# Transformer block on one core: attention with four heads on four TensorE row groups, and full-size matmuls ahead of the loop

## The reference

```python
h = _layernorm(x, axis=-1) * (1 + ca) + sa
x = x + ga * _L0_attn_ref(h, wq, w_down, wk_up, wv_up, wo)
h = _layernorm(x, axis=-1) * (1 + cb) + sb
x = x + gb * _L0_ffn_ref(h, Wg, bg, W1, b1, W2, b2)
```

```python
q = (x @ wq).reshape(B, T, H, D)
lat = x @ w_down
k = (lat @ wk_up).reshape(B, T, H, D)
v = (lat @ wv_up).reshape(B, T, H, D)
scores = jnp.einsum('bqhd,bkhd->bhqk', q, k) * scale
allowed = pages[None, :] <= pages[:, None]
scores = jnp.where(allowed[None, None], scores, jnp.finfo(scores.dtype).min)
attn = jax.nn.softmax(scores, axis=-1)
out = jnp.einsum('bhqk,bkhd->bqhd', attn, v).reshape(B, T, E) @ wo
```

## Time and profile before

| | |
|---|---|
| median of 3 runs | 771.66 us |
| the profiled execution | 771.94 us |
| its span, first to last instruction | 770.1 us |
| TensorE busy | 681.2 us (88%) |
| VectorE busy | 588.5 us (76%) |
| ScalarE busy | 520.4 us (68%) |
| GpSimd busy | 183.8 us (24%) |
| mean granted clock of TensorE | 0.940 |

### The profile page before, as it was taken

The page is one execution under the profiler, slowest core; times in us unless marked ns, Lnnn a source line. Parts: engine busy times, 40 slices in busy tenths (PEclk is TensorE's granted clock), DMA queues, the critical chain, the costliest instruction groups (busy, mean ns, idle before and its releaser), DMA issues.

```text
span 770.1 us, 12222 instructions
## 1 busy us (share of the span) xinstructions
PE 681.2 (88%) x3976; PEld 427.2 (55%) x4000; DVE 588.5 (76%) x1133; ACT 520.4 (68%) x905; POOL 183.8 (24%) x144
## 2 busy tenths in 40 slices
PE   3920988999699999987599999999999999999996
PEld 2410222333233333345478777787777877778885
DVE  5670987888588888229678898888988889888775
ACT  2530035677476777973488888888888888888984
POOL 0451016000000000000223343333433344322322
PEclk9965579999899999998799999999999999999998
DMA  9541041100101000000111110011100111101200
GB/s 237 150 139 65 0 117 40 43 21 25 46 2 44 24 20 4 3 1 1 66 45 55 56 56 28 29 56 56 55 34 24 54 56 57 54 2 55 69 15 28
DMA packets 17413, 37.20 MB, mean 48 GB/s; under 512 B 3305, under 2 KB 11241, under 8 KB 14533
## 3 DMA queue, kind: packets, MB, share of 16 engines
q1 hardware_dynamic: 16037, 34.65, 13.9%
q10 hardware_dynamic: 1312, 1.74, 0.9%
HBM read 31.86 MB, written 4.33 MB: 47 GB/s over the span
## 4 chain that ended last, share of the span: by engine, by line
PE 33%; DVE 12%; issue 5%; ACT 1%; POOL 0%; POOLq 0%; DVEq 0%
DVE gel_lo L1049 6%; PE y L952 6%; PE y L954 5%; PE y L953 5%; PE hid L943 5%; PE hid L942 5%; PE hid L941 5%; PE plog L963 2%; DVE part L1105 1%; ACT gel_hi L1017 1%; DVE at_least L1077 1%; PE pcw L972 1%; DVE cw L1096 0%; DVE cw L1094 0%; DVE dl L1084 0%
## 5 line engine op out<-in xcount | busy, mean ns | idle before, releaser
L1049 DVE TENSOR_TENSOR gel_lo<-gel,gel_hi 128x512 fp32r<-128x512 f32 x256 | 248.3, 1010 | 6.7 <-ACT gel_hi L1017 5.7
L588 DVE TENSOR_REDUCE mcol<-mx 128x1 f32<-128x512 f32 (+2 forms) x320 | 193.1, 635 | 61.7 <-PE mx L704 58.8
L562 ACT ACTIVATE probs<-st 128x512 f32<-128x512 f32 x288 | 155.7, 596 | 99.3 <-PE st L660 57.1
L1016 ACT ACTIVATE gel<-hid,b_sb 128x512 f32<-128x512 f32 x256 | 176.1, 688 | 38.5 <-PE hid L943 16.2
L1017 ACT ACTIVATE gel_hi<-hid,b_sb 128x512 fp32r<-128x512 f32 x256 | 174.7, 682 | 0.0
L1157 POOL TENSOR_TENSOR cur<-cur,part 128x512 f32<-128x512 f32 x64 | 106.4, 1663 | 250.8 <-DVE part L1105 250.8
L704 PE MATMUL mx<-ks,qs 125*128 125x512 bf16 (+3 forms) x384 | 120.8, 364 | 38.3 <-PEq L208 32.0
L952 PE MATMUL y<-gel_hi,w_hi 128*128 128x512 f32 x256 | 104.4, 408 | 0.4 <-DVE gel_lo L1049 0.2
L941 PE MATMUL hid<-cur_hi,w_hi 128*128 128x512 f32 x256 | 102.2, 399 | 0.4 <-DVE cur_lo L1123 0.4
L943 PE MATMUL hid<-cur_hi,w_lo 128*128 128x512 f32 x256 | 102.2, 399 | 0.0
L942 PE MATMUL hid<-cur_lo,w_hi 128*128 128x512 f32 x256 | 102.1, 399 | 0.0
(11 more groups left out here) (147 smaller groups left out, 521.9 us busy)
## 6 DMA issues: line engine op xcount, KB each, us to landing
cwb<-gate_rows SPq DMA_DIRECT2D x16, 1024.0 KB, 4.7
ks<-in_k_rows SPq DMA_DIRECT2D x3, 640.0 KB
qs<-in_q_rows SPq DMA_DIRECT2D x3, 616.0 KB
q_pieces<-pieces_q SPq DMA_DIRECT2D x4, 384.0 KB, 4.8
k_pieces<-pieces_k SPq DMA_DIRECT2D x4, 384.0 KB, 6.0
ks<-k_pieces SPq DMA_DIRECT2D x8, 192.0 KB
qs<-q_pieces SPq DMA_DIRECT2D x8, 192.0 KB
x_sb<-in_x SPq DMA_DIRECT2D x4, 256.0 KB, 5.2
```

The source lines that it names most:

```text
L562: nc.scalar.activation(probs[u % SLOTS][:, h, :], st[:, (HG * u + h) % ST_RING, :], ACT.Exp, scale=SCALE).then_inc(exp_done, 1)
L588: nc.vector.tensor_reduce(mcol[a % SLOTS][:, h, slot:slot + step * (len(blocks) - 1) + 1:step], mx[:, at % MX_RING, 0:len(blocks) * keys]. ...
L1016: nc.scalar.activation(gel[n % RING][:, :], hid[n % RING][:, :], ACT.Gelu_apprx_tanh, bias=bias)
L1049: nc.vector.tensor_tensor(gel_lo[n % RING][:, :], gel[n % RING][:, :], gel_hi[n % RING][:, :], ALU.subtract).then_inc(lo_ok, 1)
```

## The change

A group's four heads now lie in one tensor of 128 partitions, 32 rows a head (`HROWS`), in float32r in place of bfloat16. A head has two pieces in place of three and 3 products (24 rows), 2 rows for the maximum and 4 rows that mask by page inside one block of 128 keys. A matmul reads 24 to 30 rows of one head, so the four heads stand on four row groups of the array. The mask rows may only be read in a block on the diagonal: a matmul that crosses it is cut into one piece of 128 columns and a rest.

In the preparation GpSimd computes one remainder a side in place of two, ScalarE casts one piece a side, and SyncE issues three transfers a side and chunk in place of one. A group is loaded by two transfers of 128 rows in place of six of 24, 16 and 8 rows. After its last projection TensorE does 15 float32 matmuls of 128 by 512 (`BUSY_PREP`) into banks that nobody reads.

In the attention VectorE reads a pair of heads at a time, 20 bins a group (ring of 2 pairs). The maximum is split in two pieces, by GpSimd. UNITS has 10 units, two of them of 256 columns, and ScalarE's exponentials are as long as the unit; a unit belongs to one half of the queries, and there is one output bank in place of two. The hardware loop is gone, the code is written out. Ahead of the loop, each of the 28 pairs of bins is preceded by two full-size float32r matmuls into its own banks (`BUSY_FIRST`); `BUSY_LATER` is 0, so there are none in the loop.

```diff
-Q_PIECE = [0, 0, 0, 1, 1, 2]
-K_PIECE = [0, 1, 2, 0, 1, 0]
+Q_PIECE = [0, 0, 1]
+K_PIECE = [0, 1, 0]
 TERMS = len(Q_PIECE)
-ROW_ZERO = TERMS * D
-ROW_PAGE = 64
-ROW_MAX = P - 3
+HROWS = 32
+ROW_MAX = TERMS * D
+ROW_PAGE = ROW_MAX + 2
+ROW_END = ROW_PAGE + 4
...
-    [(0, 2, 0, 256, 256), (1, 6, 256, 256, 256)],
...
+    (0, [(2, 0, 256, 256)]),
...
+FIRST_UNIT = [0, 3]
+LAST_UNIT = [2, NU - 1]
...
+PAIRS = HG // 2
+NBINS = len(BINS) * PAIRS
+TURN_AFTER = 2 * PAIRS
+BUSY_PREP, BUSY_FIRST, BUSY_LATER = 15, 2, 0
...
-            m.ks = [ma.sb(f"ks{s}", [P, HG, T], BF16) for s in range(SLOTS)]
-            m.qs = [ma.sb(f"qs{s}", [P, HG, T], BF16) for s in range(SLOTS)]
+            m.ks = [ma.sb(f"ks{s}", [P, T], F32R) for s in range(SLOTS)]
+            m.qs = [ma.sb(f"qs{s}", [P, T], F32R) for s in range(SLOTS)]
...
 def load_group(sp, m, g, s):
...
+    for dst, src in ((m.ks[s], m.kp), (m.qs[s], m.qp)):
+        sp.dma_start(dst[:, :].bitcast(F32), src[g].rearrange("h r t -> (h r) t")).then_inc(m.qk_in[s], 16)
...
+            for rows, dst in ((w["k_rows"], m.kp), (w["q_rows"], m.qp)):
+                sp.dma_start(dst.rearrange("g h r t -> (g h) r t")[:, ROW_MAX:HROWS, :],
+                             rows.rearrange("(a r) t -> a r t", a=1).broadcast_to([GROUPS * HG, HROWS - ROW_MAX, T]))\
+                    .then_inc(in_rows, 16)
...
+                    for term, x in enumerate(which):
+                        sp.dma_start(rows[:, D * term:D * (term + 1), at],
+                                     pieces[side][:, c, x, :].bitcast(F32)).then_inc(pieces_out, 16)
...
+                    sp.wait_ge(in_rows, 32)
+                    sp.wait_ge(pieces_out, 16 * 4 * TERMS)
                     load_group(sp, m, 0, 0)
                     load_group(sp, m, 1, 1)
...
+                    pool.wait_ge(piece0, 2 * c + side + 1)
+                    nc.gpsimd.tensor_tensor(pieces[side][:, c, 1, :], ro[side][:, c % 2, :], pieces[side][:, c, 0, :],
+                                            ALU.subtract).then_inc(piece1, 1)
...
+            pe.wait_ge(h_ok, NCH)
+            for i in range(BUSY_PREP):
+                nc.tensor.matmul(turned[i % 2][:, :], m.ident[:, :], m.x[:, 0:TPC, :], start=True, stop=True)
...
-    ST_RING, MX_RING = 3, 3
-    probs = [l.sb(f"probs{s}", [P, HG, CH]) for s in range(SLOTS)]
-    ov = l.ps("ov", [P, 2, CH])
-    mx = l.ps("mx", [P, MX_RING, CH])
+    ov = l.ps("ov", [P, CH])
+    mx = l.ps("mx", [P, MX_RING, PAIRS, CH])
...
+            def max_rows(g):
+
+                s = g % SLOTS
+                sp.wait_ge(bin_read, turn_at(g) + 1)
+                for h in range(HG):
+                    n = 2 * JB
+                    sp.dma_start(m.qs[s][HROWS * h + ROW_MAX:HROWS * h + ROW_MAX + 2, :].bitcast(F32),
+                                 mrow[n * h:n * (h + 1), :]).then_inc(mrow_in[s], 16)
...
+            load_group(sp, m, 2, 2)
+            for g in range(GROUPS):
+                max_rows(g)
+                if g >= 1 and g + 2 < GROUPS:
+                    sp.wait_ge(st_done, HG * NU * g)
+                    load_group(sp, m, g + 2, (g + 2) % SLOTS)
...
+                mc = mcol[g % 2]
+                nm = mc[:, :, 0:JB]
+                hi, lo = mpc[:, :, 0, :], mpc[:, :, 1, :]
+                pool.wait_ge(mchain, CHAIN * g + 1)
+                if g >= 1:
+                    pool.wait_ge(bin_full, turn_at(g - 1) + 1)
+                nc.gpsimd.tensor_copy(hi.bitcast(F32R), nm).then_inc(mchain, 1)
+                pool.wait_ge(mchain, CHAIN * g + 2)
+                nc.gpsimd.tensor_tensor(lo.bitcast(F32R), nm, hi, ALU.subtract).then_inc(mchain, 1)
...
+            def exps(k, h):
+                u = k % NU
+                n = sum(b[3] for b in UNITS[u][1])
+                act.wait_ge(st_done, HG * k + h + 1)
+                if h == 0 and k >= PROBS:
+                    act.wait_ge(pv_done, k + 1 - PROBS)
+                nc.scalar.activation(probs[k % PROBS][:, h, 0:n], st[:, (HG * k + h) % ST_RING, 0:n], ACT.Exp,
+                                     scale=SCALE).then_inc(exp_done, 1)
+
+            def keep_output(k):
+                g, u = divmod(k, NU)
+                c = UNITS[u][0]
+                act.wait_ge(pv_done, k + 1)
+                nc.scalar.activation(m.ovs[:, g, c, :], ov[:, :], ACT.Copy).then_inc(ov_read, 1)
+            for k in range(STEPS):
                 for h in range(HG):
...
+            def merge(g):
+
+                mc = mcol[g % 2]
+                v.wait_ge(bin_read, bin_at(g, NBINS - 1) + 1)
+                nc.vector.tensor_tensor(mc[:, :, 4:8], mc[:, :, 4:8], mc[:, :, 8:12], ALU.min).then_inc(mchain, 1)
...
+            def scores(k, h):
+                g, u = divmod(k, NU)
+                s, n, r0 = g % SLOTS, HG * k + h, HROWS * h
...
+                    pe.wait_ge(m.qk_in[s], 32 * uses(g))
+                    pe.wait_ge(mrow_in[s], 16 * HG * uses(g))
+                if n >= ST_RING:
+                    pe.wait_ge(exp_done, n + 1 - ST_RING)
+                for j, off, q0, nq in blocks:
+                    own = P if j // TPC == c else 0
+                    for rows, x, w in ((ROW_END, 0, own), (ROW_PAGE, own, nq - own)):
+                        if w:
+                            mm = nc.tensor.matmul(st[:, n % ST_RING, off + x:off + x + w],
+                                                  m.ks[s][r0:r0 + rows, j * P:(j + 1) * P],
+                                                  m.qs[s][r0:r0 + rows, c * CH + q0 + x:c * CH + q0 + x + w],
+                                                  start=True, stop=True)
...
+                pe.wait_ge(exp_done, HG * (k + 1))
+                if u == 0:
+                    pe.wait_ge(vs_ok, g + 1)
+                if u in FIRST_UNIT and 2 * g + c > 0:
+                    pe.wait_ge(ov_read, 2 * g + c)
+                for j, off, q0, nq in blocks:
+                        mm = nc.tensor.matmul(ov[32 * h:32 * h + 32, q0:q0 + nq],
+                                              vs[s][:, j, h, :], probs[k % PROBS][:, h, off:off + nq],
...
+                if at >= MX_RING:
+                    pe.wait_ge(bin_read, at + 1 - MX_RING)
+                keep_busy(g, n)
                 blocks, keys, _, _ = BINS[b]
                 for x, (t, k0) in enumerate(blocks):
+                    own = P if k0 + keys == (t + 1) * P else 0
+                    for rows, y, w in ((ROW_MAX, 0, keys - own), (ROW_END, keys - own, own)):
+                        for i in range(PAIRS):
+                            r0 = HROWS * (2 * pair + i)
+                            if w:
+                                mm = nc.tensor.matmul(mx[:, at % MX_RING, i, x * keys + y:x * keys + y + w],
+                                                      m.qs[s][r0:r0 + rows, t * P:(t + 1) * P],
+                                                      m.ks[s][r0:r0 + rows, k0 + y:k0 + y + w], start=True, stop=True)
...
+            def keep_busy(g, n):
+
+                at = bin_at(g, n)
+                for i in range(BUSY_FIRST if NBINS * g + n < PAIRS * (NU + LEAD) else BUSY_LATER * (n % PAIRS == 1)):
+                    nc.tensor.matmul(mx[:, at % MX_RING, i, :], m.ks[g % SLOTS][:, 0:P], m.ks[g % SLOTS][:, 0:CH],
+                                     start=True, stop=True)
...
+                pe.wait_ge(mchain, CHAIN * (g + 1))
...
+            def bins(unit, pair):
+                g, u = divmod(unit, NU)
+                if g < GROUPS:
+                    fill_bin(g, PAIRS * u + pair)
+                if pair == PAIRS - 1 and turn_due(unit) is not None:
+                    turn_maxima(turn_due(unit))
+
+            for unit in range(NU + LEAD):
+                for pair in range(PAIRS):
+                    bins(unit, pair)
+            for k in range(STEPS):
+                scores(k, 0)
+                scores(k, 1)
+                bins(k + NU + LEAD, 0)
+                scores(k, 2)
+                if k >= 1:
+                    weigh(k - 1)
+                bins(k + NU + LEAD, 1)
+                scores(k, 3)
+            weigh(STEPS - 1)
```

More of the change, by code:

```diff
@@ L532, in _ @@
             pool.wait_ge(vs_init, 2 * SLOTS)
-            stage(0, 0)
-            stage(0, 1)
+            stage(0)
+            stage(1)
+            stage(2)
+            take_apart(0)
             pool.wait_ge(w_in, 32)
@@ L649, in _ @@
-            all_groups(v, body)
+                at = bin_at(g, n)
+                v.wait_ge(bin_full, at + 1)
+                if n == 0 and g >= 2:
+                    v.wait_ge(mchain, CHAIN * (g - 1))
+                nc.vector.tensor_reduce(mcol[g % 2][:, pair * 2:pair * 2 + 2, slot:slot + step * (len(blocks) - 1) + 1:step],
+                                        mx[:, at % MX_RING, :, 0:len(blocks) * keys].rearrange("p h (b k) -> p h b k", k=keys),
+                                        AX.X, ALU.max, negate=True).then_inc(bin_read, 1)
@@ L651, in _ @@
+            for g in range(GROUPS):
```

(46 more changed lines are left out.)

341 lines of the change are left out of this document (78 added, 263 removed).

## The result

The changed kernel takes 895.53 us (median of 4 runs, 894.28 to 897.45) against 771.57 (4 runs, 770.17 to 771.86) before: ratio 1.161, 95% interval 1.159 to 1.164, where I forecast 726 us and a range to 812. The profiled execution has a span of 894.7 us; before it was 770.1.

A forecast was written before the change was run, and what follows sets the result against it. It took the DMA queue to bound the preparation, VectorE the first maxima and TensorE the loop. 771.9 less 15 (preparation), 3 (first maxima) and 28 (loop) gave 726 us; eight in ten chances reached from 699 to 812.

The forecast's parts named there:

- Preparation: Block ahead of the first maxima: fewer subtractions and evener loads end it near 60, not 75.4, 15 us less.
- B: Rival: the clock stays at half in the loop, 35 us a group, 801 us in all (757 to 842); chance 0.28.
- The clock enters it risen: Loop: argument against a half-speed clock there, that the clock is already up when the loop starts; no size given.
- first maxima: Stretch between preparation and loop: VectorE reads two heads an instruction, 28.6 us against 31.6, 3 us less.
- Slow matmuls leave TensorE no pauses: Loop: argument against a lasting half clock, that a half-speed loop is dense; no size given.
- nothing full-size stands in the loop but the weighing: Loop: argument for a half clock, that only the weighing and one turn a group are full-size; no size given.
- the projections as a sign that few rows do no harm: Projections: the clock held 1.00 there though some use 64 rows, taken as evidence against a half-speed loop.
- A: Main case: loop at full speed, 26.1 us a group, 28 us less, 726 us in all (700 to 745); chance 0.46.
- Under the 1.02 that VectorE takes, which hides them: First maxima: added matmuls and the pair behind them take some 0.9 us at full speed, hidden by VectorE's 1.02.
- C: Rival: row groups do not overlap or 128-column pieces are dear, 31 to 34 us a group, 773 us; chance 0.14.

The follow-up runs named there:

- run 4: Changed kernel with six instead of two added full-size matmuls ahead of each of the 28 first pairs, none in the loop: 900.34 us.
- run 1: Kernel before, with the matmuls of scores and maxima reading only 32 of the 128 rows, order and waits unchanged: 928.16 us.
- run 7: Kernel before, with the matmuls of scores and maxima reading only rows 0 to 63: 927.32 us.
- Run 6: Changed kernel with the fourth head's scores of a step issued ahead of the next pair of maxima, not behind it: 869.3 us.
- run 5: Changed kernel without any added full-size matmuls, neither in the preparation nor ahead of the first pairs: 873.62 us.
- run 2: Changed kernel with every matmul of scores and maxima reading all 128 rows, so no row groups and another result: 780.41 us.
- run 3: Changed kernel with two full-size matmuls also ahead of every second pair of maxima in the loop: 890.66 us.
- run 11: Kernel before with the hardware loop over the groups written out and nothing else changed: 762.15 us.
- run 9: Kernel before with only the matmuls of the maxima on 32 rows, scores still on all rows: 869.76 us.

## Why the prediction was wrong

- **Preparation: right.** -15.2 us against -15, at 60.25 against "near 60".
- **The step that failed: which clock the loop gets.** I gave B 0.28, for two reasons that the runs refute. "The clock enters it risen": it did not, since it had fallen ahead of the first maxima and was at 0.50 all through them, and where it did enter risen it lasted some 4 us (run 4). "Slow matmuls leave TensorE no pauses": they left 41 us of pauses, and dense work on few rows stays at 0.50 all the same (run 1, 387.3 of 389.8 us busy). What stood for B, "nothing full-size stands in the loop but the weighing", was the cause. I had also read the projections as a sign that few rows do no harm; run 7 shows that this was no evidence for a loop in which two thirds of the columns have them. The Trainium skill, TensorE: Matmul & The Clock Gate, Part 1, says that sustained activity releases the throttle. These runs do not bear it out where the activity is on 24 to 64 rows, and the measurement decides.
- **B's own size: too small, 801 against 895.5.** Three terms: first maxima 53.25 us instead of 40, loop 348 instead of 270, projection 4 more, at a mean clock of 0.69 where it had 0.82; 13 + 78 + 4 = 95. In the loop I had set a full group at 35 us, between 29 and 40; it takes 44.4. As a mean of all eight TensorE is busy for 307/8 = 38.4, with 1.87 for a weighing (I had 1.71), and 5.1 us more are pauses. The round with ScalarE, which I had put into A's step, I left out of B's, as if a slow TensorE could not wait. Run 6 shows it can: 3.5 us a group go by order alone.
- **The first maxima: the cover failed.** "Under the 1.02 that VectorE takes, which hides them" holds at full clock only. With the clock at 0.50 the pair and its added matmuls take 1.87 against the 1.22 of VectorE's read of it, and leaving them out saves 22 us (run 5). With the rows full (run 2) this stretch has 37.2 us (60.3 to 97.5), still 6 more than run 5.
- **A's own size: too good.** The one piece of the loop at full clock gives some 28.3 us for a full group, not 26.1, by the estimate of run 3. With the forecast's own terms for start and end that is 8 x 28.3 - 5 + 2 = 223 us. Even with the clock kept, the loop would have given some 10 us and not 28, about what the written-out loop gives alone (run 11), and the change some 744 us in all. And without overlap, C's 31 to 34 a group was right (31.4, run 2), though its 773 was 7 too low, for the first maxima (37 us).

## What to carry over

Before packing small contractions side by side on TensorE, compare what is won with a doubled price of every column: test it by cutting the rows of the kernel that exists, an edit of four slices that gives the answer here (928 us) and needs no rewriting. When a rival doubles one engine's time, work its whole round out anew, waits included, not only that engine's sum. And of a change with several parts, ask which part's gain can be had alone: here one moved load and a written-out loop gave 18 us without touching a matmul.

## Not expected of the hardware

- Matmuls on few rows cost the clock, not only the rows: the same dense loop at 0.50 on 32 and on 64 rows (928, 927 us), at 0.96 to 0.98 on 96 (772). It happens in both types: bf16 in runs 1 and 7, float32r in the changed kernel.
- The clock has a memory. With a third of the columns on 32 rows it stayed at 1.00 for 100 us, and at 0.50 for 200 us after one pause, with the same work; it rose when that third ended (run 9). With added matmuls the same steps ran at either clock (run 3).
- Each change between row-group matmuls and full ones comes with 0.3 us that is not streaming at half clock, loading of weights included (first maxima); at full clock 0.14 was seen for the change to the weighing.
